# A graph kernel's setup on one Trainium2 core: clearing of counts, condition products, ranking, group tiles and store semaphores are moved or rewritten

## What is computed

```
edge_index = stack([src, dst])
x = x + L0(relu(layernorm(x)), edge_index, node_vec1)        # 4 blocks
x = x + L1(relu(layernorm(x)), edge_index, edge_type_2)      # 2 relation layers
# L0: cond = silu([sin(ph), cos(ph)] @ f_w1 + f_b1) @ f_w2 + f_b2,  ph = noise * freqs
#   block: y = layernorm(x) * (1 + cond @ sw + sb) + cond @ bw + bb
#          scores = q[src] . k[dst] per head; softmax over the edges of src; segment sum of v[dst]; x += y @ wo + bo
#          y = the same modulated norm; x += relu(y @ w1 + b1) @ w2 + b2
# L1: w[r] = sum_b att[r, b] * basis[b];  msg = sigmoid(x_j @ gate[r]) * x_j @ w[r];  segment sum over row, + x @ root + bias
```

## Time and profile before

| | us |
|---|---|
| median of 3 runs | 2337.94 |
| lowest, highest | 2336.54, 2338.82 |
| the profiled execution | 2339.98 |
| its span | 2338.1 |

### The profile page before, as it was taken

One profiled execution on the slowest core, in us unless ns is written; L12 is line 12 of the kernel. 1 busy time (PEld: TensorE's weight loads), 2 busy tenths in 40 slices (PEclk: granted clock), 3 DMA queues, 4 the chain that ended last, 5 costly groups with the idle time before them and its releaser, 6 DMA issues.

```text
span 2338.1 us, 36473 instructions
## 1 busy us (share of the span) xinstructions
PE 2201.4 (94%) x13797; PEld 1902.8 (81%) x13797; DVE 1594.8 (68%) x3323; ACT 1119.3 (48%) x1806; POOL 546.4 (23%) x401
## 2 busy tenths in 40 slices
PE   3889979999999999999999999999999999999998
PEld 1455658899888889988888998898899888877877
DVE  9989995478776558777656887763787774344233
ACT  5156652377733347763335775233677533231321
POOL 6000000166500026640004663000566200000000
PEclk9999979999999999999999999999999999999999
DMA  8887963111032011013102003111110421062034
GB/s 254 258 258 237 275 207 96 53 33 34 17 101 73 11 52 44 23 37 116 37 20 65 23 23 102 61 37 31 44 44 1 134 73 29 1 121 41 1 70 105
DMA packets 137379, 189.59 MB, mean 81 GB/s; under 512 B 61285, under 2 KB 61733, under 8 KB 137211
## 3 DMA queue, kind: packets, MB, share of 16 engines
q1 hardware_dynamic: 133208, 180.48, 27.8%
q10 hardware_dynamic: 4003, 6.79, 0.9%
HBM read 155.16 MB, written 32.07 MB: 80 GB/s over the span
## 4 chain that ended last, share of the span: by engine, by line
PE 75%; DVE 13%; ACT 5%; issue 5%; DVEq 1%; POOL 0%; SPq 0%; DMA 0%; ACTq 0%; POOLq 0%
PE PS L1045 10%; PE PS L1073 9%; PE PS L952 6%; PE PS L954 6%; PE PS L953 6%; PE PS L1059 6%; PE PS L938 5%; PE PS L942 4%; PE PS L939 4%; PE PS L1201 4%; PE PS L1211 4%; PE PS L859 4%; DVE chunk_hot L1675 2%; PE PS L812 1%; ACT prob L1434 1%
## 5 line engine op out<-in xcount | busy, mean ns | idle before, releaser
L793 POOL TENSOR_SCALAR prob<-prob,inv_den 125x1000 f32<-125x1000 f32 x160 | 444.4, 2777 | 0.0
L781 POOL TENSOR_TENSOR rstd<-var_eps,neg_half 125x2 f32<-125x2 f32 x45 | 35.5, 788 | 903.3 <-DVE var_eps L1597 903.3
L1434 ACT ACTIVATE prob<-prob,neg_max 125x1254 f32<-125x1254 f32 x160 | 215.5, 1347 | 56.8 <-DVE neg_max L1938 56.6
L1933 DVE CUSTOM_DVE_ANT_0 prob<-PS,sbias 125x1254 f32<-125x1254 f32 x160 | 233.0, 1456 | 11.5 <-issue 8.9
L1073 PE MATMUL PS<-pT_hi,v_hi 125*128 125x250 f32 x800 | 236.0, 295 | 0.0
L1952 DVE TENSOR_TENSOR pT_lo<-PS,pT_hi 125x1000 fp32r<-125x1000 f32 x160 | 191.1, 1194 | 50.7 <-ACT pT_hi L1451 50.7
L1073 PE MATMUL PS<-pT_lo,v_hi 125*128 125x250 f32 x800 | 224.2, 280 | 0.0
L1073 PE MATMUL PS<-pT_hi,v_lo 125*128 125x250 f32 x800 | 222.4, 278 | 0.0
L1059 PE MATMUL PS<-ident,prob 125*125 125x125 f32 x1600 | 201.2, 273 | 5.6 <-DVE pT_lo L1955 5.5
L1059 PEld LDWEIGHTS PS<-ident,prob 125*125 125x125 f32 x1600 | 195.7, 188 | 12.5 <-issue 7.5
L1449 ACT ACTIVATE pT_hi<-PS 125x1000 fp32r<-125x1000 f32 x160 | 162.0, 1012 | 82.7 <-PE PS L1059 82.7
(11 more groups left out here) (330 smaller groups left out, 5571.2 us busy)
## 6 DMA issues: line engine op xcount, KB each, us to landing
basis_t<-in_L_gnn_basis_dram SPq DMA_DIRECT2D x320, 192.0 KB, 4.2
sbias<-score_bias SPq DMA_DIRECT2D x40, 548.6 KB
adj<-adj SPq DMA_DIRECT2D x20, 546.9 KB
w_lo_raw<-in_L_gnn_m_w_dram SPq DMA_DIRECT2D x8, 1024.0 KB, 7.0
score_bias<-biases SPq DMA_DIRECT2D x10, 548.6 KB
adj<-count SPq DMA_DIRECT2D x10, 546.9 KB
xc<-x_lat SPq DMA_DIRECT2D x12, 448.0 KB
x_first<-x_lat SPq DMA_DIRECT2D x10, 448.0 KB
```

The source lines that it names most:

```text
L793: pool.tensor_scalar(prob[u % 3][:, 0:SPLIT], prob[u % 3][:, 0:SPLIT], inv_den[0:T, u % 4:u % 4 + 1], None, ALU.mult)\
L1434: act.activation(prob[u % 3][:], prob[u % 3][:], ACT.Exp, bias=neg_max[0:T, u % 4:u % 4 + 1], accum_out=den[0:T, u % 4:u % 4 + 1]).then_in ...
L1933: v.tensor_tensor_reduce(prob[u % 3][:].rearrange("p (j s) -> p j s", j=3), PS[0:T, 0:3, 0:SB], sbias[p % 2][a][:].rearrange("p (j s) -> p ...
```

## The change

1. *Clearing of `count`.* POOL clears tiles 0 to 15 only, as soon as DVE has signalled `own_ready` a second time, during the ranking; ACT clears tiles 16 to 19 with two activations of scale 0 after `node_relu`. So that `count` can be cleared then, `mask`, `cum`, `ph` and `ph_int` move out from under it into the space of the sort's buffers, and `rank` goes. DVE waits for `z1_ps` (the last reader of `ph`) before its first `place_hot`. On POOL the clearing now stands ahead of `node_scales`.
2. *Condition products.* `silu` and `cond_low` leave POOL: DVE does the product after sort batch 1 and the subtraction after batch 9.
3. *Ranks.* One `scalar_tensor_tensor` per bucket (20 of 157 columns) computes `(cum + base) * mask` in place; a tree of five additions replaces the reduction.
4. *Group tiles.* Each of 128 partitions counts how many of the 20 ends its number has reached; PE turns that column into a row in bank 7, and DVE takes the minimum. PE's transpose stands ahead of its wait for `fw_in`.
5. *Loads.* 2 or 3 relation loads a batch, 23 in all, and 52 in the counting.
6. *Stores.* `adj_stored` becomes three semaphores, for t of 0 to 3, 4 to 7, and 8 and 9; ACT waits for the first before `k_hi`, DVE for the second before `k_lo`, ACT for the third before the first `v_hi`.

```diff
-        LOADS_SORT = [2 + b % 2 for b in range(SORT_BATCHES)]
-        LOADS_COUNT = [50 * (n + 1) // NG - 50 * n // NG for n in range(NG)]
+        LOADS_SORT = [2 + (b % 3 == 2) for b in range(SORT_BATCHES)]
+        LOADS_COUNT = [52 * (n + 1) // NG - 52 * n // NG for n in range(NG)]
@@ SP
-                    sp.dma_start(adj[r0:r1, k, :], count[r0:r1, k, 0:N]).then_inc(adj_stored, 16)
+                    sp.dma_start(adj[r0:r1, k, :], count[r0:r1, k, 0:N]).then_inc(adj_stored[t // 4], 16)
@@ POOL
             node_phases()
             attention_blocks()
+            pool.wait_ge(own_ready, 2)
+            pool.memset(count[:, 0:COUNT_POOL, :].bitcast(fp32), 0.0).then_inc(count_zero, 1)
             node_scales()
-            silu()
-            pool.wait_ge(pos_ready, 1)
-            pool.wait_ge(z1_ps, 1)
-            pool.memset(count[:].bitcast(fp32), 0.0).then_inc(count_zero, 1)
-            cond_low()
-            pool.wait_ge(cond_ready, 1)
@@ PE
+            pe.wait_ge(own_ready, 2)
+            pe.transpose(PS[0:1, 7, 0:NG], group_col[0:NG, :], ident[0:NG, 0:NG]).then_inc(prefix_ps, 1)
@@ ACT
             node_relu()
+            act.wait_ge(pos_ready, 1)
+            act.wait_ge(node_no_ready, 1)
+            for k in range(COUNT_POOL, NB, 2):
+                z = act.activation(count[:, k:k + 2, :].rearrange("p k s -> p (k s)").bitcast(fp32), node_no[0:T, :], ACT.Copy, scale=0.0)
+            z.then_inc(count_zero, 1)
...
-            act.wait_ge(adj_stored, 32 * NT)
...
+                    if lay == 0 and p == 0 and a == 0:
+                        act.wait_ge(adj_stored[2], 32 * (NT - 8))
...
+                    if lay == p == 0:
+                        act.wait_ge(adj_stored[0], 32 * 4)
@@ DVE
-            link(v.tensor_tensor(base[:], ends[:], grp[:], ALU.subtract))
+            v.tensor_tensor(base[:], ends[:], grp[:], ALU.subtract)
+            link(v.tensor_scalar(reached[:], ends[:], part_no[:, 0:1], None, ALU.is_le))
+            v.tensor_reduce(group_col[:], reached[:], AX.X, ALU.add).then_inc(own_ready, 1)
...
-            link(v.tensor_tensor(rank[:], cum[:], base[:].unsqueeze(2).to_broadcast([128, NB, EC]), ALU.add))
-            link(v.tensor_tensor(rank[:], rank[:], mask[:], ALU.mult))
-            link(v.tensor_reduce(pos[:], rank[:].rearrange("p k c -> p c k"), AX.X, ALU.add))
+            for k in range(NB):
+                last = v.scalar_tensor_tensor(cum[:, k, :], cum[:, k, :], base[:, k:k + 1], mask[:, k, :], ALU.add, ALU.mult)
+            link(last)
+            for k, n in ((10, 10), (5, 5), (2, 2), (1, 1)):
+                link(v.tensor_tensor(cum[:, 0:n, :], cum[:, 0:n, :], cum[:, k:k + n, :], ALU.add))
+            link(v.tensor_tensor(pos[:], cum[:, 0, :], cum[:, 4, :], ALU.add))
...
+            v.wait_ge(prefix_ps, 2)
+            v.tensor_scalar(group_tile[:], PS[0:1, 7, 0:NG], NB - 1.0, None, ALU.min)
             v.tensor_reduce(large[:], grp[0:1, :], AX.X, ALU.max).then_inc(pos_ready, 1)
 
-            v.wait_ge(x_sums, 2 * NT + 1)
             for b in range(SORT_BATCHES):
...
+                else:
+                    v.wait_ge(z1_ps, 1)
+                    v.wait_ge(x_sums, 2 * NT + 1)
...
+                if b == 1:
+                    v.wait_ge(z1_exp, 4)
+                    v.tensor_tensor(z1[:], z1[:], z2[:], ALU.mult).then_inc(silu_done, 1)
...
+            v.tensor_scalar(large_flag[:], large[:], 4096.0 / GE, None, ALU.is_gt)
+            v.wait_ge(cond_hi, 1)
+            v.tensor_tensor(cond3[32:32 + C, :], z2[:], cond3[0:C, :].bitcast(fp32), ALU.subtract).then_inc(cond_ready, 1)
             v.wait_ge(sort_used, SORT_BATCHES)
-            v.tensor_scalar(large_flag[:], large[:], 4096.0 / GE, None, ALU.is_gt)
-            link(v.tensor_tensor(group_ge[:], group_no[:].unsqueeze(2).to_broadcast([1, NG, NB]),
-                                 ends[0:1, :].unsqueeze(1).to_broadcast([1, NG, NB]), ALU.is_ge))
-            link(v.tensor_reduce(group_no[:], group_ge[:], AX.X, ALU.add))
-            v.tensor_scalar(group_tile[:], group_no[:], NB - 1.0, None, ALU.min)
...
-            v.wait_ge(count_zero, 1)
+            v.wait_ge(count_zero, 2)
...
+                    if lay == p == 0:
+                        v.wait_ge(adj_stored[1], 32 * 4)
```

More of the change, by code:

```diff
@@ L228, in gnn_kernel @@
         bucket = m("bucket", [128, EC])
[L229 to L233, removed]
         assert m.at <= COUNT_END
@@ L251, in gnn_kernel @@
         chunk_hot = [m(f"chunk_hot{i}", [128, SORT_BATCH, TC], f16) for i in range(2)]
+        RANK_END = m.at
         node_no = m("node_no", [128, SW], f16)
-        group_no = m("group_no", [1, NG])
+        part_no = m("part_no", [128, 1])
+        reached = m("reached", [128, NB])
+        group_col = m("group_col", [128, 1])
         freq_off = m("freq_off", [F2, 4])
@@ L266, in gnn_kernel @@
         m = Map(PLACE_AT)
-        group_ge = m("group_ge", [1, NG, NB])
+        ph = m("ph", [F2, N])
+        ph_int = m("ph_int", [F2, N])
+        mask = m("mask", [128, NB, EC], bf16)
+        cum = m("cum", [128, NB, EC])
+        assert m.at <= RANK_END
         m = Map(W_OUT)
@@ L398, in gnn_kernel @@
             "consts", "edges_in", "noise_in", "fw_in", "att_in", "att_ready", "bias_cols_ps", "cols_out"))
-        (edge_pads, own_ready, prefix_ps, pos_ready, place_done, sort_hot, sort_used, sort_ps, phase, sin_done,
+        (edge_pads, own_ready, prefix_ps, pos_ready, place_done, sort_hot, sort_used, phase, sin_done,
          z1_ps, z1_exp, silu_done, z2_ps, cond_hi, cond_ready, basis_out, basis_used, row_of_ready,
          x_sums, x_var, x_scaled, h0_ready, count_zero) = map(plain, (
-             "edge_pads", "own_ready", "prefix_ps", "pos_ready", "place_done", "sort_hot", "sort_used", "sort_ps", "phase",
+             "edge_pads", "own_ready", "prefix_ps", "pos_ready", "place_done", "sort_hot", "sort_used", "phase",
              "sin_done", "z1_ps", "z1_exp", "silu_done", "z2_ps", "cond_hi", "cond_ready",
@@ L408, in gnn_kernel @@
         w_stored = [plain(f"w_stored{i}") for i in range(4)]
-        (hot_ready, group_out, count_ps, count_added, node_no_ready, csum_ready, csumT_ps, logs_ready, sbias_ready,
-         adj_stored) = map(plain, (
+        (hot_ready, group_out, count_ps, count_added, node_no_ready, csum_ready, csumT_ps, logs_ready,
+         sbias_ready) = map(plain, (
              "hot_ready", "group_out", "count_ps", "count_added", "node_no_ready", "csum_ready", "csumT_ps", "logs_ready",
-             "sbias_ready", "adj_stored"))
+             "sbias_ready"))
+        adj_stored = [plain(f"adj_stored{i}") for i in range(3)]
         sbias_stored = [plain(f"sbias_stored{i}") for i in range(4)]
@@ L718, in _ @@
                       allow_small_or_imprecise_dtypes=True).then_inc(consts, 1)
[L719 removed]
+            pool.iota(part_no[:], [[0, 1]], base=0, channel_multiplier=1,
                       allow_small_or_imprecise_dtypes=True).then_inc(consts, 1)
@@ L1644, in _ @@
             v.tensor_tensor(own[:], cum[:, :, EC - 1], cum_before[:], ALU.subtract).then_inc(own_ready, 1)
-            v.scalar_tensor_tensor(edge_dst[:, 0:EC], tile_f[:], -float(T), dst_f[:], ALU.mult, ALU.add)
+            link(v.scalar_tensor_tensor(edge_dst[:, 0:EC], tile_f[:], -float(T), dst_f[:], ALU.mult, ALU.add))
             v.wait_ge(prefix_ps, 1)
```

1 line of the change is left out of this document (added).

## The result

The changed kernel takes 2316.66 us in the median of 4 executions (2313.29 to 2320.19) against 2337.24 us of the kernel before (4 executions, 2334.5 to 2338.82). The ratio is 0.9909, 95% interval 0.9897 to 0.9921: 20.6 us faster. In a second set, five executions of the changed kernel and nine of the kernel before, it took 2320.28 us against 2339.6, ratio 0.9914 (0.9898 to 0.9929). The forecast was 2315.2, range 2310 to 2323.5.

The account below looks back on a forecast made before the run. DVE was taken to bound the setup before the first attention tile, PE from about 360 us on. Terms summed to 22.7 us, giving 2317.3 from the profiled 2339.98 and 2315.2 from the median 2337.94; range 2310 to 2323.5.

Parts of the forecast that it names:

- memset's old place: Sort batch 1: its 16 chunk_hot stood for GpSimd's memset; moving it saves 8.04 us (10.92 less 2.88).
- cond_low: Sort's end: dst_place's stall goes, gaining 2.6 us; DVE's 1.45 us subtraction hides in its 2.59 us wait for PE.
- PE warm: Counting's start: without the group tiles PE idles less before the first group, gaining 1.9 us (0 to 2.4).
- store semaphores: First projection: ACT's wait for the last adj store goes; PE restarts 1.6 us earlier, clock 0.7, together 2.3 us.
- between 0.18 and 0.31 I take 0.25: Ranking: us assumed per scalar_tensor_tensor of 157 columns, so 5.0 us (3.6 to 6.2) for the 20.
- I take no stall: Ranking: the rank operations and most of the tree lose nothing beside GpSimd's memset in its new place.
- rival B: Ranking: the memset locks DVE out of everything until 35.6 us; 7.6 us less gain, 2322.8 us; chance 0.12.
- Most of it is start and end, so 0.4: Counting: two loads moved in from the sort cost 0.4 us (0 to 2.5), as most DVE idle lies elsewhere.
- rival C: Sort: basis loads run dry once the memset stall that fills the ring goes; 5 us back, about 2320; chance 0.10.
- D: Sort's end: PE stays at its low clock, losing the 1.9 us and some 2 more; 2319 us; chance 0.07.
- E: Counting: it runs at PE's low clock; 20 pairs of groups give 27 us lost, 2365 us; chance 0.03.
- F: Whole kernel: the gain is taken back in an unseen wait; within 0.2%, 2338 us; chance 0.03.

Follow-up runs that it names:

- POOL clears 2: Changed kernel with GpSimd clearing 2 tiles of count instead of 16 and ScalarE 18; the 20 rank operations took 5.95 us, slot_src at 106.41 us.
- PE busy: Changed kernel with group tiles made after the sort and 18 matmuls added on TensorE before the first group; first 12 matmuls 2.31 us, slot_src at 110.94 us.
- Old loads: Changed kernel with the earlier dealing of relation loads, 25 in the sort and 50 in the counting; slot_src at 111.83 us, counting 183.44 us.
- wv behind k: Changed kernel with DVE's wv_lo subtraction moved behind k_lo for layer 0; median 2314.8 us, ratio to the kernel before 0.9888.
- changed, again: Changed kernel repeated unchanged in five rounds; 2320.28 us against 2339.6 for the kernel before, ratio 0.9914; first v_hi at 349.40 us.
- clearing late: Changed kernel with GpSimd's clearing of 16 tiles put back behind pos_ready and the SiLU's exponentials; slot_src at 113.69 us.
- ranks whole: Changed kernel with the ranks again made by three operations over 3140 columns; pos_c at 40.13 us, slot_src at 110.06 us.
- products on POOL: Changed kernel with both condition products back on GpSimd; slot_src at 111.77 us.

## Why the prediction was right

The time, 2316.66, is 1.5 above the forecast of 2315.2, and the sum of 22.7 stands against 22.3 at the marks and 20.6 in the medians. Term by term, from the two traces and the experiments:

| term | forecast | measured | from |
|---|---|---|---|
| ranking, small operations, node_scales | 3.2 - 0.5 | 2.4 | first `chunk_hot` 41.14 to 38.78 |
| memset's old place | 8.0 | 8.0 | 10.92 to 2.88 |
| SiLU product | 1.1 | 1.1 | 3.73 to 1.23, less 1.36 |
| cond_low | 2.6 | 2.65 | 3.79 to 1.14, the operation hidden |
| group tiles | 4.5 | 4.7 | last `dst_place` to `slot_src` 7.22 to 2.52 |
| PE warm, less the loads | 1.9 - 0.4 | 1.8 - 0.8 | DVE's waits for PE in the counting 2.42 to 0.58, the rest of it 181.75 to 182.56 |
| store semaphores | 2.3 | 2.4 | last addition to first `v_hi` 62.80 to 60.39 |

*Ranking.* The step that failed in size is "between 0.18 and 0.31 I take 0.25": it measured 0.298, 5.96 instead of 5.0 for the twenty. The row of one such operation, 0.31, was nearly the answer; the `chunk_hot` at 0.18 are of another type and mode. The tree took 4.05 as worked out (33.24 to 37.29). node_scales cost 0 instead of 0.5: GpSimd waited, not DVE.

*The memset's new place.* "I take no stall" held, shown by changing its size ("POOL clears 2"), and rival B fell. By the Trainium skill, SBUF — State Buffer, section "Who interferes with whom", an instruction with two SBUF inputs doesn't collide with a GpSimd instruction that only writes, and tensor_scalar can. The traces agree: `dst_place` 1.22 and the ranks 5.96 beside a memset, 16 `chunk_hot`, which are tensor_scalar, 9.40.

*cond_low.* It cost nothing, as the wait still had 1.00 left. That cover is thin: the gap between DVE's last `dst_place` and `slot_src` is 2.5 us, and it is as long as PE's last 26 matmuls take (2.44).

*PE warm.* That the first groups were slow by the clock is shown ("PE busy"). DVE waited for PE twice at the start of the counting before, 1.61 and 0.81 (the 2.4 of the earlier trace rows), and waits once now, 0.58: 1.8 less, against 1.9 forecast. The counting shortened by only 1.0 all the same, and the reason lies in the next term.

*Loads.* Here the step "Most of it is start and end, so 0.4" was too small: the counting without DVE's waits for PE grew by 0.8 in these two traces and by 1.1 in the mean of all, and it is shorter still with 49 loads ("Old loads"). That is inside the 0 to 2.5 that I had allowed. The sign of the edit as a whole was wrong too. I weighed it only by what it adds to the counting and put the basis transfers into rival C with 0.10. Both belonged together: without this edit C happens. In this the number owes something to luck: all terms up to `slot_src` are counted at DVE's pace in the sort, and the sort keeps that pace only by the edit that I had booked as a small cost. The rival's own condition, the stall that lets the ring fill, fits the traces: with the same dealing of loads PE's weight loads waited 0.6 us for basis data in the sort of the kernel before, and 9.4 without the stalls.

*Stores.* 1.6 for PE's first `q` column was right: from the modulation's second operation it comes after 1.63 instead of 3.30. The other 0.75 lie between the first `q` column and the first `v_hi` (10.61 instead of 11.36), where the granted clock is 0.87 instead of 0.80.

*D, E and F* didn't happen: from 85 to 120 us the granted clock of the changed kernel is 1.00.

## What to carry to other kernels

When a GpSimd instruction lies beside a VectorE piece that is several times as long as its kind, look at what both touch: clearing memory by GpSimd was free beside two-tensor operations and cost its whole remaining length beside 16-bit tensor_scalar, and a small product was cheaper on VectorE than the wait it caused. When a stall is removed, ask what had caught up during it: here the transfers had, and a dealing of loads that was harmless before would have taken back 5.1 of 19 us. Judge such an edit by marks in the trace, as single executions of the changed kernel differed by up to 8 us, while its marks repeated to 0.1 up to `slot_src` and to 0.7 up to the first `v_hi`.

## What was not expected of the hardware

*A spread of 4.6 us outside the change.* The 1966 us behind the first `v_hi` took 1961.4 or 1961.5 in three traces and 1965.7 to 1966.3 in ten, the same kernel in both groups; only "wv behind k", with 1968.1, lies apart. Windows near the same work in the kernel before and in the first profile of the changed one (columns as above):

```profile
455.00:475.00 20.00, 16.35 (x91) 14.54 (x90) 13.47 (x36) 13.68 (x22) 11.80 (x8) 0.91 0.22 63
```

```profile
430.00:450.00 20.00, 16.36 (x97) 14.44 (x96) 13.08 (x36) 14.51 (x23) 11.42 (x8) 1.00 0.22 64
```

PE is busy for 16.35 and 16.36 of 20 us, but the granted clock is 0.91 in one and 1.00 in the other. The slower group has three such dips: here, once more between 1921 and 1950 us and once more between 2115 and 2144, at a place that moves with the length of the setup. Each costs about 1.5 us; the faster group has none. Before the second PE idles for 1.5 us between two stages in "changed, again"; but it is just as busy there as in the first profile of the same kernel, which has no dip (15.54 of 17 us over 1905 to 1922 in both). Why an execution falls into one group or the other isn't settled.

*PE as the sort's bound.* DVE never waits for PE in the sort of the changed kernel, only behind its last batch. But where the low clock falls late in the sort, 0.9 to 1.6 us are lost on top of what was undone: in "clearing late" and "ranks whole" the 32 matmuls of batch 7 take 4.1 instead of 2.9 us, in "products on POOL" the last 26 take 4.08 instead of 2.44.

*GpSimd waits for a row of short instructions.* In "clearing late" the node scales stand beside the ranks. Their last product, 0.21 us in the changed kernel, was issued at 29.09 and took 4.20: it ended at 33.29, as the last of the 20 rank operations did, 33.23, though each of these takes only 0.298. It was not let in between two of them, and they lost nothing (5.95). In "POOL clears 2" the same product was issued at 30.78, later in the same row, and ended with it too:

```profile
28.71 1.99 POOL L756 TENSOR_TENSOR xrstd<-xsq,half 125x10 f32<-125x10 f32 x1
30.78 2.54 POOL L758 TENSOR_TENSOR xnmr<-xrstd,xneg 125x10 f32<-125x10 f32 x1
```

By the Trainium skill, SBUF — State Buffer, section "Who interferes with whom", an instruction with two SBUF inputs collides with a GpSimd instruction that reads, the shared ports are an exclusive lock, and the order of issue decides who blocks. For this product the traces agree, but for the length: the block lasted for the whole row of instructions. For the power ahead of it they don't: it reads two tensors as well, was issued at 28.71 in the middle of the ranks, and took 1.99 us, no more than the 1.98 that it takes beside a reduction in "ranks whole". What sets the two apart isn't shown.
